# Local attention on Trainium2: the softmax matrix P transposed in one piece, with the work around it in another order

## The chip, the core and the metric

The kernel runs on one core of a Trainium2 chip. The metric is device time in microseconds (us): the median of a few executions. One further execution was profiled, and everything read from the trace comes from it.

## The reference

The input is 8 sequences of 256 tokens with 128 features. A first attention (8 heads of 16) with layer norms and a modulation comes first. Then each sequence passes six layers of local attention and a gated feed-forward block, and this is nearly all of the time:

```python
q = l2norm(q) * qs;  k = l2norm(k) * ksc          # 16 heads of 64
q = q * cos * scale + rotate_half(q) * sin * scale  # rope
k = k * cos * inv + rotate_half(k) * sin * inv
sim = einsum('bhwie,bhwje->bhwij', bq, bk2) * 8.0   # windows of 32, each sees 64 keys
attn = softmax(where(mask, -inf, sim))
x = (attn @ v) @ Wo + x
# feed-forward, 128 -> 2 x 341 -> 128
a, gate = split(layernorm(shift(x)) @ W1 + b1)
x = a * gelu(gate) @ W2 + b2 + x
```

Everything is float32 in result. The kernel gets there with matmuls in float32, and for the projections with operands split in a high and a low part (`x_hi`, `x_lo`, `wqkv_hi`, `wqkv_lo`, `w1_hi`, `w1_lo`).

## The kernel before

The six layers of eight sequences are 48 "slots" (`SLOTS`), one for each layer and sequence, numbered g. There are five programs, one for each engine: TensorE (`pe`), VectorE (`dve`), ScalarE (`act`), GpSimd (`pool`) and SyncE (`sp`, for the DMAs). Each is written out by hand, and each engine takes its instructions in this order. No scheduler moves anything; engines meet only at semaphores (`wait_ge`, `then_inc`). Waits count from `CREDIT`.

A slot has two halves, for m = 0 and m = 1, which are the two blocks of 128 tokens of the sequence. Work of several slots lies in one slot:

- attention of slot g: `scores` (TensorE), `centre` (VectorE subtracts the row maximum), `exps` (ScalarE), `turn_p` (TensorE transposes P), `copy_p` (ScalarE copies P from PSUM), `attend` (TensorE, P times V), `normalise` (VectorE), `turn_o`, `copy_o`;
- of slot g + 1 the projections `q`, `k`, `v`, their rope (`rope_products` on VectorE, `rotate` on GpSimd), the norms, and `turn_k`, `turn_q`;
- of slot g - 1 the output projection `project_out`, the `residual` and the statistics of the layer norm (`mean`, `variance`);
- of slot g - 3 (`LAG`) the feed-forward: `gates_up`, `gates`, `values_up`, `products`, `down`, `add`.

PSUM has eight banks, all in use. Banks 4 and 5 take the transposed P: in the kernel before four heads' pairs at a time (`turn_p(g, m, 0)`, then `turn_p(g, m, 1)`). The second piece goes over the first, so it waits for the copy of the first (`p_copied`). `attend` waits for the copy of the second. In the first half one half of `project_out` stands between the two pieces; in the second half `down` does.

The waits of the first half that matter here are these (lines of the kernel before):

- `k(g + 1, 0)` (L694) writes banks 6 and 7 and waits for the first of the gates, which is read from bank 7;
- `rope_products(g + 1, 0, 1)` on VectorE (L1418 and L1422) reads the projection of K and waits for `k_proj`;
- `values_up` (L857 to L864) waits for the gates and, for its last part in bank 0, for `att_done`, which the residual (L1466) gives;
- `products` (L1484) waits for the values;
- `turn_k(g, 1)` writes banks 0 and 1, so it waits for the products, and `turn_q(g, 1)` writes banks 4 and 5, so it waits for the first `normalise` (L1458), which reads `attend`'s result there:

```python
pe.wait_ge(s["f_prod"], CREDIT + 3 * (pair - LAG) + 3)     # turn_k, m = 1
pe.wait_ge(s["o_normed"], CREDIT + 2 * n - 1)              # turn_q
```

In the second half `attend(g, 1, 1)` writes banks 2 and 3 and waits for `square_of(g + 1, 1, 0)` (L1060, ScalarE), and `variance` (L833) writes bank 2 and waits for the last `normalise` of the half. At the end of a layer ScalarE also rounds the next layer's weights (`round_weights`, L990, in slots 6 and 7 of a layer; `round_up`, L995, in slot 2).

ScalarE's tables: `gates` needs the table with Gelu; the exponentials need the other. Each slot loads each once (L1157, L1159).

Of the kernel before, what the change touches and what calls it, by code (L numbers as in the profile page):

```python
# [35 lines left out]
H, D = 16, 64  # L36
INNER = H * D
W = 32
SPAN = 64
# [27 lines left out]
def build(nc, xT, w1s, w2s, w3T, woT, cT, wmod, wqkv, scales, wo, params, w1, w2, consts, out):  # L67
    with ExitStack() as ctx:
# [469 lines left out]
        def _(pe):  # L538
# [55 lines left out]
            def turn(bank, c, src):  # L594


                width = src.shape[1]
                for t in range(2):
                    r = slice(64 * t, 64 * t + 64)
                    mm = pe.transpose(ps[0:width, bank + t, 64 * c:64 * c + 64], src[r], ident[r, r],  # L600
                                      tile_position=(64 * t, 0))
                return mm
# [165 lines left out]
                                           tile_position=(D * c, W * w))  # L768
                mm.then_inc(s["scored"], 1)

            def turn_p(pair, m, g):
                n = 2 * pair + m
                if g == 0:
                    pe.wait_ge(s["centred"], CREDIT + 2 * n + 2)
                else:
                    pe.wait_ge(s["p_copied"], CREDIT + 2 * n + 1)
                pe.wait_ge(s["exped"], CREDIT + 2 * n + g + 1)
                pe.sem_inc(s["pe_waited"], 1)
                for hh in range(4):
                    mm = turn(4, hh, s_sb[:, g, 2 * hh:2 * hh + 2, :].rearrange("p c k -> p (c k)"))  # L780
                mm.then_inc(s["p_turned"], 1)

            def attend(pair, m, g, over_q=True):

                n = 2 * pair + m
                if g == 0:
                    pe.wait_ge(s["v_moved"], CREDIT + 16 * (18 * pair + 8 + 10 * m))
                    pe.wait_ge(s["p_copied"], CREDIT + 2 * n + 2)
# [14 lines left out]
                mm.then_inc(s["attended"], 1)  # L803
# [6 lines left out]
                    mm = turn(2, c, o_n[:, P * c:P * c + P])  # L810
                mm.then_inc(s["o_turned"], 1)

            def project_out(pair, half):

                if half == 0:
                    pe.wait_ge(s["o_copied"], CREDIT + 2 * pair + 2)
                    pe.wait_ge(s["w_a_loaded"], 16 * layer_of(pair) + 16)
                    pe.wait_ge(s["centred"], CREDIT + 4 * pair + 5 if not isinstance(pair, int) or pair < SLOTS - 1
                               else CREDIT + 4 * pair + 4)
                for c in range(4 * half, 4 * half + 4):  # L820
                    mm = pe.matmul(ps[:, 0, 0:N], wo_sb[:, c, :], o_t[:, c, :], start=(c == 0),  # L821
                                   stop=(c == H // 2 - 1), skip_group_check=True)
                if half:
                    mm.then_inc(s["projected"], 1)

            def mean(f, bank=1):
                pe.wait_ge(s["f_shifted"], CREDIT + 2 * f + 2)
# [58 lines left out]
            def slot(g, out=True, ff=True, ahead=True):  # L886
# [3 lines left out]
                    q(g + 1, 0)  # L890
                if ff:
                    gates_up(g - LAG)
                if out:
                    project_out(g - 1, 0)
                if ahead:
                    k(g + 1, 0, gates=ff)
                turn_p(g, 0, 0)
                if out:
                    project_out(g - 1, 1)
                turn_p(g, 0, 1)  # L900
                if ff:
                    values_up(g - LAG)
                attend(g, 0, 0)
# [9 lines left out]
                if ahead:  # L913
                    q(g + 1, 1)
                    k(g + 1, 1)
                turn_p(g, 1, 0)
                if ff:
                    down(g - LAG)
                turn_p(g, 1, 1)
                if out:  # L920
                    mean(g - 1)
                attend(g, 1, 0)
# [36 lines left out]
            project_out(SLOTS - 1, 0)  # L959
            project_out(SLOTS - 1, 1)  # L960
# [12 lines left out]
        def _(act):  # L973
# [129 lines left out]
            def copy_p(pair, m, g):  # L1103
                n = 2 * pair + m
                act.wait_ge(s["p_turned"], CREDIT + 2 * n + g + 1)
                act.wait_ge(s["attended"], CREDIT + 2 * n)
                act.activation(p_t[:, 4 * g:4 * g + 4, :].rearrange("p c (t k) -> p t c k", t=2),  # L1107
                               pair_of_banks(2)[:, :, 0:4 * SPAN].rearrange("p t (c k) -> p t c k", c=4),
                               ACT.Copy)\
                   .then_inc(s["p_copied"], 1)  # L1110

            def copy_o(pair, m):
# [40 lines left out]

            def slot(g, ff=True, norm=True, out=True, ahead=True, more=True, after=None, layer=None):

                if ff:
                    act.preload_act_table_set("gelu_and_others")  # L1157
                    gates(g - LAG)
                    act.preload_act_table_set("natural_log_exp_and_others")  # L1159
                exps(g, 0, 0)  # L1160
                if after == 7:
                    round_weights(layer, 2)
                copy_p(g, 0, 0)
                exps(g, 0, 1)
                if ahead:
                    high(g + 1, 1)
                copy_p(g, 0, 1)
                if ahead:
                    square_of(g + 1, 0, 0)
                    square_of(g + 1, 0, 1)  # L1170
# [7 lines left out]
                    inverse_norms(g + 1, 0)  # L1178

                exps(g, 1, 0)  # L1180
                if norm:
                    round_norm(g - 2)
                if after == 6:
                    round_weights(layer, 0)
                if after == 2:
                    round_up(layer)
                copy_p(g, 1, 0)
                exps(g, 1, 1)
                if more:
                    high(g + 2, 0)  # L1190
                copy_p(g, 1, 1)
                if after == 6:
                    round_weights(layer, 1)
                if ahead:
                    square_of(g + 1, 1, 0)
                if out:
# [67 lines left out]
        def _(dve):  # L1264
# [172 lines left out]
            def centre(pair, m, g):  # L1437
# [8 lines left out]
                dve.wait_ge(s["p_turned"], CREDIT + 2 * n)  # L1446
# [48 lines left out]
            def slot(g, out=True, ff=True, ahead=True):  # L1495
                centre(g, 0, 0)
                centre(g, 0, 1)
                if ahead:
                    rope_products(g + 1, 0, 0)
                    rope_products(g + 1, 0, 1)  # L1500
                if out:
                    residual(g - 1)
                if ff:
                    products(g - LAG)
                normalise(g, 0, 0)
# [139 lines left out]
```

## Time and profile before

| | |
|---|---|
| median of three executions | 1722.73 us (1717.05 to 1724.04) |
| profiled execution, its own time | 1714.45 us |
| span of the profiled execution | 1712.6 us |
| busy: TensorE, VectorE, ScalarE, GpSimd | 94%, 78%, 75%, 62% of the span |
| granted clock of TensorE, mean | 0.980 |
| chain of waits: TensorE, issue, ScalarE, VectorE | 89%, 5%, 3%, 2% of the span |
| DMA engines busy, mean | 27.3% for the main queue |

The span runs from the first to the last instruction; the execution's own time is 1.85 us more. A busy TensorE means that a matmul was running, not that it ran at its peak. The clock is a share of 2.4 GHz, and 0.5 is 1.2 GHz. The chain of waits goes back from the last instruction, at each step to what released it; when a piece of it is an engine's own instruction, the engine waited for nothing.

### The profile page before, as it was taken

The page shows a single profiled execution, that of the slowest core. Times are in us where ns is not written, and L with a number is a line of the kernel's source. Part 1 is how long each engine was busy: PE and PEld are TensorE (multiplying, and loading weights), DVE is VectorE, ACT ScalarE, POOL GpSimd, SP SyncE. Part 2 cuts the span into 40 slices and gives each one's busy share as a digit, 9 for nine tenths or more (in the row PEclk, how much of TensorE's full clock was granted, in tenths as well). Part 3 has the DMA queues.
Part 4 walks back from the last instruction along what each step waited for, and adds up shares of the span by engine and source line. Part 5 has one row for each costly group of instructions (what it writes and reads, how often), then busy time and mean ns, then how long its engine had stood idle before and what let it go on. Part 6 is the DMA issues. An engine that isn't in the chain of part 4 may idle for free.

```text
span 1712.6 us, 89331 instructions
## 1 busy us (share of the span) xinstructions
PE 1613.6 (94%) x36892; PEld 1250.3 (73%) x36892; DVE 1333.5 (78%) x1952; ACT 1282.2 (75%) x2104; POOL 1066.3 (62%) x783
## 2 busy tenths in 40 slices
PE   7896688999999999999999999999999999999996
PEld 3574567777777777777777777777777777777775
DVE  5576667787888878888888888887887888888863
ACT  4794456788787778877778777788777788787873
POOL 2202656568676768666668667678676677776641
PEclk9898899999999999999999999999999999999998
DMA  2000423222422322423322422223322222332220
GB/s 99 2 0 1 131 52 74 54 68 68 129 69 54 72 69 58 125 64 73 72 49 70 129 69 62 61 71 76 107 68 71 68 65 74 72 73 66 65 57 26
DMA packets 75728, 116.79 MB, mean 68 GB/s; under 512 B 17294, under 2 KB 27276, under 8 KB 74764
## 3 DMA queue, kind: packets, MB, share of 16 engines
q1 hardware_dynamic: 75660, 115.99, 27.3%
q8 instruction: 30, 0.49, 0.1%
q14 instruction: 38, 0.31, 0.1%
HBM read 19.04 MB, written 1.05 MB: 12 GB/s over the span
## 4 chain that ended last, share of the span: by engine, by line
PE 89%; issue 5%; ACT 3%; DVE 2%; DMA 0%; POOL 0%; ACTq 0%; DVEq 0%; SPq 0%
PE ps L600 15%; PE ps L821 10%; PE ps L714 10%; PE ps L799 9%; PE ps L764 9%; PE ps L718 8%; PE ps L717 8%; PE ps L882 4%; PE ps L757 3%; PE ps L843 2%; PE ps L845 2%; PE ps L844 2%; PE ps L833 2%; PE ps L828 2%; PE ps L589 1%
## 5 line engine op out<-in xcount | busy, mean ns | idle before, releaser
L412 POOL TENSOR_TENSOR arena<-arena,rnorm 128x1024 f32<-128x1024 f32 x192 | 361.8, 1906 | 347.6 <-ACT rnorm L1071 347.6
L403 POOL TENSOR_TENSOR arena<-arena 128x1024 f32<-128x1024 f32 x192 | 457.0, 2380 | 16.1 <-DVE arena L1422 12.4
L600 PEld LDWEIGHTS ps<-cst,arena 64*128 64x128 f32 x6656 | 243.3, 140 | 148.9 <-issue 140.1
L600 PE MATMUL ps<-cst,arena 64*128 64x64 f32 x6656 | 300.3, 230 | 25.2 <-ACT arena L1101 9.4
L1418 DVE TENSOR_TENSOR arena<-ps,rope 128x1024 f32<-128x1024 f32 x192 | 234.5, 1221 | 90.7 <-issue 79.8
L1107 ACT ACTIVATE arena<-ps 128x512 f32<-128x512 f32 x192 | 114.7, 597 | 174.3 <-PE ps L600 174.0
L1422 DVE TENSOR_TENSOR arena<-ps,rope 128x1024 f32<-128x1024 f32 x192 | 232.9, 1213 | 0.0
L718 PE MATMUL ps<-wqkv_hi,x_hi 128*128 128x512 f32 x576 | 230.0, 399 | 0.0
L717 PE MATMUL ps<-wqkv_lo,x_hi 128*128 128x512 f32 x576 | 229.4, 398 | 0.0
L1432 DVE TENSOR_REDUCE norm<-arena 128x16 f32<-128x1024 f32 x192 | 224.2, 1208 | 0.0
L714 PE MATMUL ps<-wqkv_hi,x_lo 128*128 128x512 f32 x576 | 214.8, 454 | 9.2 <-issue 7.5
L1443 DVE TENSOR_REDUCE rmax<-ps 128x8 f32<-128x512 f32 x192 | 131.7, 686 | 106.4 <-PE ps L764 105.9
L1060 ACT ACTIVATE arena<-ps 128x1024 f32<-128x1024 f32 x192 | 190.3, 1020 | 9.0 <-DVE arena L1422 9.0
L799 PE MATMUL ps<-v_sb,arena 64*32 64x66 f32 x12288 | 165.6, 227 | 26.2 <-issue 10.6
L821 PE MATMUL ps<-arena,wo_sb 128*128 128x256 f32 x768 | 186.7, 386 | 1.2 <-issue 1.2
L799 PEld LDWEIGHTS ps<-v_sb,arena 64*32 64x32 f32 x12288 | 138.1, 106 | 63.4 <-issue 52.0
L764 PE MATMUL ps<-k_t,arena 64*32 64x64 f32 x12288 | 165.7, 224 | 6.0 <-issue 6.0
L764 PEld LDWEIGHTS ps<-k_t,arena 64*32 64x32 f32 x12288 | 134.1, 105 | 29.9 <-issue 6.9
L1087 ACT ACTIVATE k_t<-ps 128x1024 f32<-128x1024 f32 x96 | 98.4, 1025 | 75.4 <-PE ps L600 73.2
L821 PEld LDWEIGHTS ps<-arena,wo_sb 128*128 128x128 f32 x768 | 139.0, 190 | 19.8 <-issue 1.3
L1447 DVE TENSOR_TENSOR arena<-ps,rmax 128x512 f32<-128x512 f32 x192 | 132.7, 691 | 15.2 <-DVE rmax L1443 0.7
L1458 DVE TENSOR_TENSOR arena<-ps,rden 128x512 f32<-128x512 f32 x192 | 132.7, 691 | 14.7
(122 smaller groups left out, 2745.4 us busy)
## 6 DMA issues: line engine op xcount, KB each, us to landing
v_sb<-v_nat SPq DMA_DIRECT2D x576, 130.0 KB, 2.4
v_sb<-v_nat SPq DMA_DIRECT2D x192, 65.0 KB, 2.0
wqkv_sb<-wqkv SPq DMA_DIRECT2D x6, 1536.0 KB, 6.4
v_sb<-v_sb SPq DMA_DIRECT2D x96, 65.0 KB, 2.0
wo_sb<-wo SPq DMA_DIRECT2D x6, 512.0 KB, 8.1
w_sb<-w SPq DMA_DIRECT2D x6, 341.0 KB, 7.8
x<-xT SPq DMA_DIRECT2D x1, 1024.0 KB, 5.0
scl<-scales SPq DMA_DIRECT2D x6, 128.0 KB, 7.6
```

What stands on the lines that cost most here:

```text
L403: pool.tensor_tensor(t_cos[:, m, j, :], t_cos[:, m, j, :], t_sin[:, j, :], ALU.add)\
L412: pool.tensor_tensor(x, x, rnorm[:, H * j:H * j + H].unsqueeze(2).to_broadcast([P, H, D]), ALU.mult).then_inc(s[done], 1)
L600: mm = pe.transpose(ps[0:width, bank + t, 64 * c:64 * c + 64], src[r], ident[r, r], tile_position=(64 * t, 0))
L714: pe.matmul(ps[:, bank + c, :], x_lo[:, m, :], wqkv_hi[:, w], start=True, stop=False)
L717: pe.matmul(ps[:, bank + c, :], x_hi[:, m, :], wqkv_lo[:, w], start=False, stop=False)
L718: mm = pe.matmul(ps[:, bank + c, :], x_hi[:, m, :], wqkv_hi[:, w], start=False, stop=True)
L764: mm = pe.matmul(ps[W * w:W * w + W, 4 * g + c, SPAN * hh:SPAN * hh + SPAN], q_t[r, 4 * g + hh, W * w:W * w + W], k_t[r, 4 * g + hh, P * m ...
L799: mm = pe.matmul(ps[W * w:W * w + W, 4 - 2 * g + c, ON * hh:ON * hh + ON], p_t[r, h, W * w:W * w + W], v_sb[r, m, w, VD * h:VD * h + ON], ...
L821: mm = pe.matmul(ps[:, 0, 0:N], wo_sb[:, c, :], o_t[:, c, :], start=(c == 0), stop=(c == H // 2 - 1), skip_group_check=True)
L1418: dve.tensor_tensor(t_cos[:, m, j, :].rearrange("p (h d) -> p h d", h=H), src.rearrange("p a (h d) -> p (a h) d", h=8), tc.unsqueeze(1).to ...
L1422: dve.tensor_tensor(t_sin[:, j, :].rearrange("p (h s d) -> p h s d", h=H, s=2), src.rearrange("p a (h s d) -> p (a h) s d", h=8, s=2)[:, : ...
L1432: dve.tensor_reduce(norm2[:, H * j:H * j + H], sq[:, j, :].rearrange("p (h d) -> p h d", h=H), AX.X, ALU.add).then_inc(s["normed"], 1)
```

## The change

P is transposed in one piece of eight pairs of heads into all of banks 4 and 5, and copied by one instruction. On TensorE this stands directly behind `gates_up`, ahead of the output projection (which is now one piece), of K and of the values; in the second half it stands ahead of `down`. On ScalarE both `exps` and the copy come first, then the gates with their two table loads, and in the second half the roundings, `high(g + 2, 0)` and `round_norm` come after the copy. On VectorE the `residual` stands ahead of the rope of K.

```diff
@@ TensorE, a slot
                 if ff:
                     gates_up(g - LAG)
+                turn_p(g, 0)
                 if out:
-                    project_out(g - 1, 0)
+                    project_out(g - 1)
                 if ahead:
                     k(g + 1, 0, gates=ff)
-                turn_p(g, 0, 0)
-                if out:
-                    project_out(g - 1, 1)
-                turn_p(g, 0, 1)
                 if ff:
                     values_up(g - LAG)
                 attend(g, 0, 0)
...
-                turn_p(g, 1, 0)
+                turn_p(g, 1)
                 if ff:
                     down(g - LAG)
-                turn_p(g, 1, 1)
                 if out:
                     mean(g - 1)
@@ TensorE, turn_p
-                if g == 0:
-                    pe.wait_ge(s["centred"], CREDIT + 2 * n + 2)
-                else:
-                    pe.wait_ge(s["p_copied"], CREDIT + 2 * n + 1)
-                pe.wait_ge(s["exped"], CREDIT + 2 * n + g + 1)
+                pe.wait_ge(s["centred"], CREDIT + 2 * n + 2)
+                pe.wait_ge(s["exped"], CREDIT + 2 * n + 2)
@@ ScalarE, a slot
+                exps(g, 0, 0)
+                exps(g, 0, 1)
+                copy_p(g, 0)
                 if ff:
                     act.preload_act_table_set("gelu_and_others")
                     gates(g - LAG)
                     act.preload_act_table_set("natural_log_exp_and_others")
-                exps(g, 0, 0)
                 if after == 7:
                     round_weights(layer, 2)
-                copy_p(g, 0, 0)
-                exps(g, 0, 1)
                 if ahead:
                     high(g + 1, 1)
-                copy_p(g, 0, 1)
...
                 exps(g, 1, 0)
+                exps(g, 1, 1)
+                copy_p(g, 1)
+                if more:
+                    high(g + 2, 0)
                 if norm:
                     round_norm(g - 2)
                 if after == 6:
                     round_weights(layer, 0)
+                    round_weights(layer, 1)
                 if after == 2:
                     round_up(layer)
-                copy_p(g, 1, 0)
-                exps(g, 1, 1)
-                if more:
-                    high(g + 2, 0)
-                copy_p(g, 1, 1)
-                if after == 6:
-                    round_weights(layer, 1)
                 if ahead:
                     square_of(g + 1, 1, 0)
@@ VectorE, a slot
                 if ahead:
                     rope_products(g + 1, 0, 0)
-                    rope_products(g + 1, 0, 1)
                 if out:
                     residual(g - 1)
+                if ahead:
+                    rope_products(g + 1, 0, 1)
                 if ff:
                     products(g - LAG)
```

On TensorE, in the first half of a slot of the main loop, this stood in a row before (L821 the output projection, L714 to L718 K, L600 the transposes of P):

```order
L821 MATMUL ps<-arena,wo_sb 128x256 x4
L696 REGISTER_ALU
L699 ISA
L714 MATMUL ps<-wqkv_hi,x_lo 128x512 x2
L717 MATMUL ps<-wqkv_lo,x_hi 128x512
L718 MATMUL ps<-wqkv_hi,x_hi 128x512
L717 MATMUL ps<-wqkv_lo,x_hi 128x512
L718 MATMUL ps<-wqkv_hi,x_hi 128x512
L774 ISA
L777 REGISTER_ALU
L600 MATMUL ps<-cst,arena 128x64 x8
L821 MATMUL ps<-arena,wo_sb 128x256 x4
```

At the same place in the changed kernel stands this (L818 is its output projection):

```order
L774 ISA
L600 MATMUL ps<-cst,arena 128x64 x16
L813 ISA
L814 ISA
L815 ISA
L818 MATMUL ps<-arena,wo_sb 128x256 x8
L696 REGISTER_ALU
L699 ISA
L714 MATMUL ps<-wqkv_hi,x_lo 128x512 x2
L717 MATMUL ps<-wqkv_lo,x_hi 128x512
L718 MATMUL ps<-wqkv_hi,x_hi 128x512
L717 MATMUL ps<-wqkv_lo,x_hi 128x512
```

The 16 transposes are in one run, and K has moved behind the whole output projection: four float32 matmuls and the transposes that stood behind it now stand ahead of it.

On VectorE, in the same half, the products of rope (L1418, L1422), the residual (L1466) and the gated products (L1484) stood so before:

```order
L1418 TENSOR_TENSOR arena<-ps,rope 128x1024
L1422 TENSOR_TENSOR arena<-ps,rope 128x1024
L1415 REGISTER_ALU
L1418 TENSOR_TENSOR arena<-ps,rope 128x1024
L1422 TENSOR_TENSOR arena<-ps,rope 128x1024
L1465 REGISTER_ALU
L1466 REGISTER_ALU x2
L1466 ISA
L1466 TENSOR_TENSOR h<-ps,h 128x256
```

In the changed kernel the lines are 13 lower:

```order
L1405 TENSOR_TENSOR arena<-ps,rope 128x1024
L1409 TENSOR_TENSOR arena<-ps,rope 128x1024
L1452 REGISTER_ALU
L1453 REGISTER_ALU x2
L1453 ISA
L1453 TENSOR_TENSOR h<-ps,h 128x256
L1402 REGISTER_ALU
L1405 TENSOR_TENSOR arena<-ps,rope 128x1024
L1409 TENSOR_TENSOR arena<-ps,rope 128x1024
```

The residual has moved from behind the second pair of rope products (K's) to ahead of it; the gated products and `normalise` follow that pair now.

## Rows read from the trace of the kernel before

**Rows 1.** Busy time in one slot: us, PE PEld DVE ACT POOL, PEclk, DMA share, GB/s.

```profile
940.36:971.05 30.69, 30.44 (x740) 24.02 (x740) 25.47 (x36) 24.05 (x39) 20.52 (x15) 1.00 0.53 149
```

**Rows 2.** The chain of waits, first half of that slot: start us, us, what.

```profile
940.36 0.24 PE ps L757 x4
...
945.17 1.73 PE ps L821 x8
...
948.30 0.39 PE ps L600 x8
948.69 1.92 PE ps L821 x8
...
951.01 0.32 PE ps L843
...
952.27 1.64 PE ps L799 x102
953.92 1.14 PE ps L600 x32
955.05 0.66 PE ps L714 x2
...
956.65 0.64 PE ps L600 x16
957.29 0.23 PE ps L757 x4
```

**Rows 3.** The chain of waits, the same slot's second half.

```profile
962.77 1.49 PE ps L882 x6
...
966.25 0.11 issue
966.36 0.85 PE ps L799 x49
...
968.35 0.66 PE ps L833 x2
...
971.05 0.23 PE ps L757 x4
```

**Rows 4.** The timeline of VectorE, first half: start us, us, instruction, idle before.

```profile
948.48 1.22 DVE L1418 TENSOR_TENSOR arena<-ps,rope 128x1024 f32<-128x1024 f32 x1 [1.80 <-issue]
...
950.93 0.42 DVE L1466 TENSOR_TENSOR h<-ps,h 128x256 f32 x1
951.96 1.26 DVE L1484 SCALAR_TENSOR_TENSOR f_a<-ps,par,f_a 128x256 f32<-128x256 f32 x3 [0.60 <-PE ps L845]
...
953.46 0.69 DVE L1458 TENSOR_TENSOR arena<-ps,rden 128x512 f32<-128x512 f32 x1
```

**Rows 5.** The timeline of VectorE, second half (first and last of 14 rows).

```profile
958.35 0.69 DVE L1443 TENSOR_REDUCE rmax<-ps 128x8 f32<-128x512 f32 x1 [0.90 <-PE ps L764]
...
967.56 0.69 DVE L1458 TENSOR_TENSOR arena<-ps,rden 128x512 f32<-128x512 f32 x1
```

**Rows 6.** The timeline of ScalarE in that slot.

```profile
942.74 1.28 ACT L1157 ACT_TABLE_LOAD   x1
944.49 0.47 ACT L1151 ACTIVATE f_a<-ps,par 85x256 f32<-85x256 f32 x1 [0.47 <-PE ps L845]
...
965.19 1.02 ACT L1060 ACTIVATE arena<-ps 128x1024 f32<-128x1024 f32 x1
```

**Rows 7.** The chain of waits, a slot that rounds weights.

```profile
902.92 1.06 ACT wqkv_hi L990
```

**Rows 8.** The timeline of TensorE, between slots 0 and 1.

```profile
215.88 1.03 PE L600 MATMUL ps<-cst,arena 64*128 64x64 f32 x27 [1.82 <-issue]
...
217.69 0.63 PE L717 MATMUL ps<-wqkv_lo,x_hi 128*128 128x512 f32 x1
```

**Rows 9.** The page's costliest groups: busy us, mean ns of one | idle before.

```profile
L717 PE MATMUL ps<-wqkv_lo,x_hi 128*128 128x512 f32 x576 | 229.4, 398 | 0.0
```

**Rows 10.** The timeline of TensorE, first slot of a loop pass.

```profile
545.67 0.46 PE L600 MATMUL ps<-cst,arena 64*128 64x64 f32 x8 [1.10 <-ACT arena L1101]
```

More of the change, by code:

```diff
@@ L769, in scores, with turn_p @@
                 mm.then_inc(s["scored"], 1)
-            def turn_p(pair, m, g):
+            def turn_p(pair, m):
                 n = 2 * pair + m
-                if g == 0:
-                    pe.wait_ge(s["centred"], CREDIT + 2 * n + 2)
-                else:
-                    pe.wait_ge(s["p_copied"], CREDIT + 2 * n + 1)
-                pe.wait_ge(s["exped"], CREDIT + 2 * n + g + 1)
+                pe.wait_ge(s["centred"], CREDIT + 2 * n + 2)
+                pe.wait_ge(s["exped"], CREDIT + 2 * n + 2)
                 pe.sem_inc(s["pe_waited"], 1)
-                for hh in range(4):
-                    mm = turn(4, hh, s_sb[:, g, 2 * hh:2 * hh + 2, :].rearrange("p c k -> p (c k)"))
+                for h in range(H // 2):
+                    mm = turn(4, h, s_sb[:, h // 4, 2 * (h % 4):2 * (h % 4) + 2, :].rearrange("p c k -> p (c k)"))
                 mm.then_inc(s["p_turned"], 1)
@@ L787, in attend @@
                     pe.wait_ge(s["v_moved"], CREDIT + 16 * (18 * pair + 8 + 10 * m))
-                    pe.wait_ge(s["p_copied"], CREDIT + 2 * n + 2)
+                    pe.wait_ge(s["p_copied"], CREDIT + n + 1)
                     pe.sem_inc(s["pe_waited"], 1)
@@ L811, in turn_o, with project_out @@
                 mm.then_inc(s["o_turned"], 1)
[L813 to L820, printed above, removed]
+            def project_out(pair):
+                pe.wait_ge(s["o_copied"], CREDIT + 2 * pair + 2)
+                pe.wait_ge(s["w_a_loaded"], 16 * layer_of(pair) + 16)
+                pe.wait_ge(s["centred"], CREDIT + 4 * pair + 5 if not isinstance(pair, int) or pair < SLOTS - 1
+                           else CREDIT + 4 * pair + 4)
+                for c in range(H // 2):
                     mm = pe.matmul(ps[:, 0, 0:N], wo_sb[:, c, :], o_t[:, c, :], start=(c == 0),
                                    stop=(c == H // 2 - 1), skip_group_check=True)
-                if half:
-                    mm.then_inc(s["projected"], 1)
+                mm.then_inc(s["projected"], 1)
             def mean(f, bank=1):
@@ L958, in _ @@
             pe.wait_ge(s["f_done"], CREDIT + SLOTS - LAG)
-            project_out(SLOTS - 1, 0)
-            project_out(SLOTS - 1, 1)
+            project_out(SLOTS - 1)
             down(SLOTS - 3, 7)
@@ L1101, in exps, with copy_p @@
                 act.activation(v, v, ACT.Exp).then_inc(s["exped"], 1)
-            def copy_p(pair, m, g):
+            def copy_p(pair, m):
                 n = 2 * pair + m
-                act.wait_ge(s["p_turned"], CREDIT + 2 * n + g + 1)
+                act.wait_ge(s["p_turned"], CREDIT + n + 1)
                 act.wait_ge(s["attended"], CREDIT + 2 * n)
-                act.activation(p_t[:, 4 * g:4 * g + 4, :].rearrange("p c (t k) -> p t c k", t=2),
-                               pair_of_banks(2)[:, :, 0:4 * SPAN].rearrange("p t (c k) -> p t c k", c=4),
-                               ACT.Copy)\
+                act.activation(p_t.rearrange("p c (t k) -> p t c k", t=2),
+                               pair_of_banks(2).rearrange("p t (c k) -> p t c k", c=8), ACT.Copy)\
                    .then_inc(s["p_copied"], 1)
@@ L1445, in centre @@
                 dve.wait_ge(s["maxed"], CREDIT + 2 * n + g + 1)
-                dve.wait_ge(s["p_turned"], CREDIT + 2 * n)
+                dve.wait_ge(s["p_turned"], CREDIT + n)
                 dve.tensor_tensor(s_sb[:, g, :, :].rearrange("p (h a) k -> p a h k", a=2), src,
```

## The prediction

> **What bounds the kernel now.** I read the granted clock and the busy time of one slot first, then the chain of waits through it, then the timelines of VectorE and ScalarE beside it. In the steady part TensorE is busy for 30.44 of a slot's 30.69 us at full clock [rows 1]. The chain of waits goes from scores to scores (940.36 to 971.05) nearly always through TensorE's own instructions; the first half takes 957.29 - 940.36 = 16.93 us, the second 13.76 [rows 2, 3]. So TensorE is the bound, with little waiting in it. What the chain doesn't say is how near the others are, and this change moves what the others wait for. That is what has to be worked out: where TensorE gets shorter, and which engine is then late.
>
> **What TensorE saves.** P is turned in two pieces, each between two full-array jobs. A run of 8 transposes takes 0.39 us, of 16 0.64 (turn_o), of 32 1.14 [rows 2]: 0.14 us to enter and 0.031 for each. The float32 passes behind transposes take 1.92 us for 8 (half an output projection) and 1.49 for 6 (down) [rows 2, 3], thus 0.215 a pass and 0.20 to enter; the same 8 passes behind another full matmul take 1.73. The values' first matmul takes 0.32 behind transposes, where I take 0.12 behind a full one. Joining the pieces removes one entry of each kind in each half: 0.14 + 0.20 = 0.34, say 0.35 us. If that were all, the first half would be 16.58 us.
> The Trainium skill (TensorE: Matmul & The Clock Gate, "Step-by-step: what each phase is for") says that weight loads are pulled ahead of running matmuls unless their row groups conflict. By that alone the joints could be free and the saving zero; the 1.92 against 1.73 us [rows 2] says that they are not, and the row decides.
>
> **The first half: who is late.** Count from the end of gates_up (945.17). On TensorE, in the new order: 16 transposes 0.64, the whole output projection 1.92 + 8 x 0.215 = 3.64, K 948.30 - (945.17 + 1.73) = 1.40: K is ready at +5.68, where it was ready at +3.13. Behind it: values 1.26 - 0.20 = 1.06, attend 1.65, and turn_k would begin at +8.39 and turn_q, 16 transposes later (0.64), at +9.03.
> VectorE can only begin K's rope products when K is there. It began 0.18 us after K's end (948.48 against 948.30); the pair takes 2.45 us to the next instruction (950.93); the three gated products begin at 951.96 and last 1.26; the first normalise behind them is over at 953.46 + 0.69 = 954.15, that is 2.19 us after the products' start [rows 4]. Before, the residual and the wait for the values lay between; there the gated products ended at 953.22 and TensorE came to turn_k only at 953.92: 0.7 us of slack. Now nothing lies between, but all of it begins 2.55 us later. With 0.10 us for the signal ([rows 3]: 0.11 of "issue" before attend's second piece):
> - products ready for turn_k at 5.68 + 0.18 + 2.45 + 1.26 + 0.10 = +9.67, against +8.39 that TensorE would need: it waits 1.28 us;
> - normalise ready for turn_q at 5.68 + 0.18 + 2.45 + 2.19 + 0.10 = +10.60, against +9.03: 1.57 us late in all (0.3 of it after turn_k).
> From there 0.50 (the second 16 of 32 transposes), v 956.65 - 955.05 = 1.60 and turn_o 0.64 lead to the scores at +13.34. They were at 957.29 - 945.17 = +12.12. So the first half gets 1.22 us longer: 0.35 saved, 1.57 lost.
> The residual ahead of the rope costs nothing: the projection ends at +4.28, the residual takes 0.42 [rows 4], and it lies in VectorE's wait for K. The delay of K is the price, not the residual.
> P's own chain is short enough. Centre begins 1.06 us behind the start of the scores (958.35 against 957.29) [rows 2, 5] and takes four instructions of 0.69; the last exponential is half as wide as the 1.02 us of the square [rows 6], so some 0.6. That is 4.5 us, and gates_up ends at 945.17 - 940.36 = 4.81, because ScalarE no longer loads a table ahead of it. I put the wait at 0; with signals it could be up to 0.2, and it would count in full.
>
> **The second half.** The same joint saves 0.35 us of TensorE. But VectorE works there from 958.35 to 967.56 + 0.69 = 968.25 with no idle note on the 13 rows after the first [rows 5], and variance, which waits for its last instruction, begins at 968.35 [rows 3]. VectorE's work is tied to the scores and is not made shorter. So at most 0.05 us is gained, whatever TensorE saves; the bounds are 0 and 0.35. I take 0.05, the row's.
>
> **What is special.** Five slots round two pieces of weights. A 1024-wide rounding takes 1.06 us [rows 7]. Before, one was hidden in ScalarE's wait for P and one was on the path; now both stand ahead of the square that attend's second piece waits for: I count 0.8 us for each slot, 4 us (0 to 5). The six slots that round W1 get 0.3 each, 2 us (0 to 4). Slots 1 and 2, which have no feed-forward, also have K behind the projection: 1 us each. The last slot has no K and loses two waits for P: -3 (0 to -4). DMAs: none is added, and v's moves are tied to copy_v, which keeps its distance to the scores.
>
> **Sum.** 44 slots (3 to 46) x (1.22 - 0.05) = 51.5; with 4 + 2 + 2 - 3 = 5 it is 56.5 us. From the profiled execution's 1714.45 us this gives 1771. The median of the runs shown is 8 us above that execution; I go half of the way and say 1776 us, 3% slower. (What a measurement can tell from no change is about 0.5%, 8 us.)
>
> **The rivals.**
> 1. *TensorE's saving counts and VectorE does not hold it.* That is what the chain of waits by itself suggests, since it is nearly all TensorE. Then 45 slots x 0.70 = 31 us go: 1684 to 1692 us. Against it: rope products can't read K before K is there, and the 2.45 + 2.19 us behind it are measured. It would need VectorE to get there 1.6 us earlier. 8%.
> 2. *Saving and wait cancel.* For a change within 8 us a slot may gain or lose 0.18 us, so the wait would have to be 0.2 to 0.6 us, and not 1.57: 1715 to 1730 us. Even with turn_k's wait alone and the whole second joint saved it is 1.28 - 0.70 = 0.58 a slot, 26 us, 1740; that is the low end of my forecast, not this rival. 5%.
> 3. *The clock falls too.* TensorE gets pauses of 1.3 and 0.3 us in each slot. After a pause of 1.82 us the matmuls of the projection take 0.63 us, where they take 0.40 in the mean [rows 8, 9]: this is the lower level, 1.2 GHz. After one of 1.10 us the transposes run at the full one [rows 10]: 0.46 us for 8. The new pauses lie between. A fall costs about 1.7 us (0.2 us on each of eight or nine such matmuls; that so many are hit is an estimate, from the stretch between those two slots). One slot in three: 15 x 1.7 = 25 us, 1800; each slot: 75 us, 1850. 13%. The Trainium skill (TensorE: Matmul & The Clock Gate, "HAM oscillation — how this bites in real kernels") describes this: a loop with a wait in each pass may begin every pass at the lower clock. [...]
> 4. *The gates get late.* They stand behind the copy of P and a table load now, and K waits for the first. P turned at +0.64, copied in 1.02 [rows 6], table 1.28, first gate 0.47: +3.5 with the signals, while K can begin at +4.28. There is 0.8 us of slack. If it were used up, K would come later, and each 0.1 us of it costs 4 us. 4%, about 1790.
>
> **Chances and range.** My forecast 70% (1750 to 1800), rivals 1 to 4: 8, 5, 13 and 4%. Faster by over 0.5%: 8%; within 0.5%: 5%; slower: 87%. The range from 1742 takes in rival 2's 26 us and no special slots at the low end, and up to 1806 a fall of the clock in a slot of three; beyond it lie rival 1 and the worse part of 3, about 2 in 10.
>
> **What would show it.** In the profile after: the first half 18.1 to 18.2 us between the scores, the second 13.7; transposes of P in runs of 16 with 0.64 us; K's rope products starting 0.2 us after K, and the gated products directly behind them; VectorE as releaser ahead of turn_k and turn_q with about 1.3 and 0.3 us; in the chain VectorE's share far above its 2%; ScalarE's gates over before K begins. The granted clock stays at 1.00 in the steady part; lower values there would speak for rival 3. The prediction is wrong if TensorE does not wait ahead of turn_k, or if the first half is under 17 us.

## The result and the profile after

The changed kernel takes 1768.7 us (1764.8 to 1775.1, four runs), the kernel before 1719.9 us on the same chip: a ratio of 1.030, with a 95% interval of 1.027 to 1.033. It is 3% slower, and the forecast was 1776 (1742 to 1806). The profiled execution took 1767.6 us, its span is 1765.8, and the mean granted clock 0.978.

Slot times below are differences between starts of the first scores of each half, on TensorE's timeline. They repeat within 0.03 us in the plain slots:

| us | before | after | after - before |
|---|---|---|---|
| first half, plain slot | 16.93 | 18.11 | +1.18 |
| second half, plain slot | 13.76 | 13.67 | -0.09 |
| second half, slots 14, 22, 30, 38 (two roundings) | 14.82 | 16.8 | +2.0 |
| second half, slots 10, 18, 26, 34, 42 (W1) | 13.76 | 14.15 | +0.4 |
| first half, slots 11, 19, 27, 35 (first of a loop pass) | 18.4 to 18.6 | 19.6 to 19.8 | +1.2 |
| slots 0 to 3 together | | | -7.5 |

The 53.2 us by which the span grew are 43 slots (4 to 46) by 1.09 = 46.9, 8.8 more in the five slots that round two pieces of weights, 2.4 in those that round W1 and 0.5 in the others; slots 0 to 3 give 7.5 back, the start costs 2.5 and the end gives 0.4. The fifth of the slots with two roundings is slot 6: it went from 14.82 to 15.36 us only (see experiment 6).

Busy times of one plain slot of the kernel after (slot 24), in the columns of [rows 1]:

```profile
962.93:994.71 31.78, 30.09 (x743) 24.35 (x739) 25.31 (x36) 24.28 (x37) 20.51 (x15) 1.00 0.51 144
```

TensorE's busy time fell from 30.44 to 30.09 us while the slot grew to 31.78: its work got shorter, and it now waits 1.69 us. The chain through the first half of that slot says where, to be read against [rows 2]:

```profile
967.78 0.64 PE ps L600 x16
968.42 3.65 PE ps L818 x16
972.07 0.47 PE ps L714 x2
...
973.24 0.24 PE ps L718
...
975.92 1.26 DVE f_a L1471 x3
977.19 0.25 issue
977.44 0.71 PE ps L600 x16
978.16 0.71 PE ps L600 x16
978.87 0.66 PE ps L714 x2
...
980.46 0.64 PE ps L600 x16
981.10 0.23 PE ps L757 x2
```

P is turned in 0.64 us, the projection takes 3.65, K begins at 972.07. Then the chain leaves TensorE: it goes through VectorE's rope products (many small pieces and "issue", left out here) to the three gated products (975.92) and back to TensorE's transposes of K at 977.44 and of Q at 978.16, each 16 of them in 0.71, where 32 took 1.14 in one go before. VectorE's timeline of the slot, to be read against [rows 4, 5]:

```profile
972.39 0.42 DVE L1453 TENSOR_TENSOR h<-ps,h 128x256 f32 x1 [3.09 <-PE ps L818]
973.65 1.22 DVE L1405 TENSOR_TENSOR arena<-ps,rope 128x1024 f32<-128x1024 f32 x1 [0.84 <-PE ps L718]
974.79 1.22 DVE L1409 TENSOR_TENSOR arena<-ps,rope 128x1024 f32<-128x1024 f32 x1
975.92 1.25 DVE L1471 SCALAR_TENSOR_TENSOR f_a<-ps,par,f_a 128x256 f32<-128x256 f32 x3
977.10 0.19 DVE L1442 RECIPROCAL rden<-ps 128x8 f32<-128x8 f32 x1
977.32 0.69 DVE L1445 TENSOR_TENSOR arena<-ps,rden 128x512 f32<-128x512 f32 x1
...
982.16 0.69 DVE L1430 TENSOR_REDUCE rmax<-ps 128x8 f32<-128x512 f32 x1 [0.84 <-PE ps L764]
...
990.21 0.20 DVE L1442 RECIPROCAL rden<-ps 128x8 f32<-128x8 f32 x1
990.45 0.69 DVE L1445 TENSOR_TENSOR arena<-ps,rden 128x512 f32<-128x512 f32 x1
...
991.29 0.69 DVE L1445 TENSOR_TENSOR arena<-ps,rden 128x512 f32<-128x512 f32 x1
```

VectorE is idle for 3.09 us ahead of the residual and 0.84 ahead of K's rope. From there on it has no gap up to the second half's row maximum at 982.16, which waits 0.84 us for the scores, and none behind that to the end of the half. Before, it waited 0.60 us for the values ahead of the same products. The waits of TensorE (engine, line, releaser, us in total, times, longest):

```profile
PE ps L600 <- DVE f_a L1471: 51.1, 44, 1.3
PE ps L797 <- ACT arena L1051: 30.7, 46, 2.3
```

The first is the new wait: 1.24 to 1.27 us in the plain slots, 1.16 in the mean, since it is only 0.5 in the five slots that round a third piece of weights. Before, the largest wait of TensorE in that list was 10.6 us in all. The second was not foreseen: attend's second piece waits for a square of ScalarE in each second half, 0.37 us in the plain slots, 1.03 where W1 is rounded and 2.26 where two pieces are. The 0.37 cost nothing: in experiment 6 the square comes earlier, this wait is gone, and the half takes the same 13.67 us. In the page's chain TensorE's share fell from 89 to 71%:

```profile
PE 71%; issue 9%; DVE 8%; ACT 7%; POOL 2%; DVEq 1%; ACTq 1%; DMA 0%; SPq 0%; POOLq 0%
```

ScalarE in the first half, against [rows 6]:

```profile
968.54 1.02 ACT L1098 ACTIVATE arena<-ps 128x1024 f32<-128x1024 f32 x1 [0.98 <-PE ps L600]
969.58 1.28 ACT L1150 ACT_TABLE_LOAD   x1
970.87 1.20 ACT L1141 ACTIVATE f_a<-ps,par 85x256 f32<-85x256 f32 x3
```

The gates end at 972.07, when K begins; K waits for the first of the three only.

### The profile page after: what moved, and what is told of

Read it like the earlier page. It is cut to its first block, busy times and chain, and to the rows that moved or that the text cites. A ratio compares the mean times of both kernels' runs of the same rounds, so it can differ in the third digit from the quotient of the medians.

```text
span 1765.8 us, 88923 instructions
## 1 busy us (share of the span) xinstructions
PE 1599.6 (91%) x36892; PEld 1267.7 (72%) x36892; DVE 1326.8 (75%) x1952; ACT 1291.2 (73%) x2008; POOL 1065.7 (60%) x783
## 3 DMA queue, kind: packets, MB, share of 16 engines
HBM read 19.04 MB, written 1.05 MB: 11 GB/s over the span
## 4 chain that ended last, share of the span: by engine, by line
PE 71%; issue 9%; DVE 8%; ACT 7%; POOL 2%; DVEq 1%; ACTq 1%; DMA 0%; SPq 0%; POOLq 0%
PE ps L600 14%; PE ps L818 10%; PE ps L714 9%; PE ps L764 8%; PE ps L718 7%; PE ps L717 7%; DVE f_a L1471 3%; PE ps L797 3%; DVE arena L1409 2%; PE ps L757 2%; ACT arena L1051 2%; PE ps L829 2%; PE ps L589 2%; ACT f_hi L1132 1%; PE ps L839 1%
## 5 line engine op out<-in xcount | busy, mean ns | idle before, releaser
L600 PEld LDWEIGHTS ps<-cst,arena 64*128 64x128 f32 x6656 | 246.8, 141 | 164.8 <-issue 149.6
L600 PE MATMUL ps<-cst,arena 64*128 64x64 f32 x6656 | 294.4, 231 | 75.6 <-DVE f_a L1471 51.1
L1051 ACT ACTIVATE arena<-ps 128x1024 f32<-128x1024 f32 x192 | 195.3, 1017 | 58.6 <-DVE arena L1409 56.9
L718 PE MATMUL ps<-wqkv_hi,x_hi 128*128 128x512 f32 x576 | 228.8, 397 | 0.0
L714 PE MATMUL ps<-wqkv_hi,x_lo 128*128 128x512 f32 x576 | 215.1, 455 | 7.8 <-issue 7.2
L1092 ACT ACTIVATE arena<-arena 128x512 f32<-128x512 f32 x192 | 121.1, 633 | 96.8 <-DVE arena L1434 81.9
L818 PE MATMUL ps<-arena,wo_sb 128*128 128x256 f32 x768 | 180.3, 388 | 1.2 <-issue 1.2
L1098 ACT ACTIVATE arena<-ps 128x1024 f32<-128x1024 f32 x96 | 98.4, 1025 | 107.0 <-PE ps L600 107.0
L818 PEld LDWEIGHTS ps<-arena,wo_sb 128*128 128x128 f32 x768 | 143.2, 191 | 22.3 <-issue 1.3
```

Of the source, the lines that this page charges most:

```text
L714: pe.matmul(ps[:, bank + c, :], x_lo[:, m, :], wqkv_hi[:, w], start=True, stop=False)
L718: mm = pe.matmul(ps[:, bank + c, :], x_hi[:, m, :], wqkv_hi[:, w], start=False, stop=True)
L1051: act.activation(sq[:, j, :], pair_of_banks((1, 3)[j]).rearrange("p a b -> p (a b)"), ACT.Square).then_inc(s["squared"], 1)
```

## The experiments

Each edit is shown against the kernel named with it, and against the kernel after where none is named. The kernel before took 1717.3 us beside experiments 1 to 4, 1714.2 beside 5 to 8 and 1715.7 beside 9 to 11.

**1. K ahead again, the joint of the first half alone.** The output projection is in two halves, and P is turned in one piece between them; the second half is that of the kernel before.

```diff
                 if out:
-                    project_out(g - 1)
+                    project_out(g - 1, 0)
                 if ahead:
                     k(g + 1, 0, gates=ff)
+                turn_p_all(g, 0)
+                if out:
+                    project_out(g - 1, 1)
```

> The kernel before, with P in one piece in the first half alone and K where it was: output projection's first half, K, 16 transposes of P, second half of the projection, values. Both exponentials stand ahead of the gates, the copy of P behind them; the second half of the slot and VectorE's order are as before. Theory (K's delay is the whole loss, the joint a real saving): K is ready at +3.1 us after gates_up as before, the gated products are over before TensorE reaches turn_k, and the first half gets shorter by the joint: 16.93 - 0.35 = 16.58 us, second half 13.76; 44 slots x 0.35 = 15 us less, about 0.99 of before. Rival (the single piece itself, or the exponentials ahead of the gates, costs): the first half stays over 16.9 us or nears 18.1.

Measured: 1731.2 us, ratio 1.010 (1.007 to 1.013). The plain first half took 17.06 us, the second 13.76. So 1.05 of the 1.18 us came back. This kernel differs from the kernel after in the place of the residual and in ScalarE's order too, so by itself it does not single out K's place; experiments 3 and 4 and the chain do. The joint brought nothing here, against the 0.35 us of the theory. The projection ended later than before, the residual began at 607.29, and the values' last part waited for it (TensorE went on at 607.77):

```profile
607.29 0.43 DVE L1481 TENSOR_TENSOR h<-ps,h 128x256 f32 x1 [0.35 <-PE ps L830]
```

It also has one thing that neither theory holds: the first slot of each loop pass took 22.3 to 22.5 us, where ScalarE stood still for 4.76 us with nothing to wait for in the records:

```profile
536.56 1.15 ACT L1109 ACTIVATE arena<-arena 128x512 f32<-128x512 f32 x2 [4.76 <-issue]
```

The same slots took 18.5 us before; four of them are 15 us, as much as this kernel's whole distance to the kernel before.

**2. The joint of the second half alone.** The first half is that of the kernel before, the second that of the kernel after.

```diff
-                turn_p(g, 1, 0)
+                turn_p_all(g, 1)
                 if ff:
                     down(g - LAG)
-                turn_p(g, 1, 1)
```

> The kernel before with only the second half of the slot changed as in the changed kernel (P in one piece ahead of down, exponentials and copy first, roundings and high behind them). Theory: first half 16.93 us as before; second half 13.67 as in the changed kernel, bound by VectorE's unbroken work and not by TensorE (which alone would give 13.41); in the four slots that round weights after the first layer, ScalarE's two roundings hold attend's second piece and the second half is 16.8 us instead of 14.8. Sum about -3.5 us for the plain slots, +10 for the rounding ones, some +3 for W1's: 5 to 10 us above before. Rival (the first half's delay also shapes the second half): 13.7 and 16.8 would not appear here.

Measured: 1734.2 us in one execution, 17 above before where 5 to 10 were expected; plain slots 16.92 and 13.75. The slots with two roundings took 15.4 to 17.0 us in the second half, as expected in the main. The joint gives the plain second half nothing, not even the 0.09 us of the kernel after that the theory had forecast. What gives those is on VectorE. With P in two pieces in either half, the count of its copies is two for each half, and the program holds a register instruction between the first reciprocal and the multiplication behind it:

```text
194 L1455 RECIPROCAL rden<-ps 128x8 [waits attended]
195 L1457 REGISTER_ALU [waits recip]
196 L1458 TENSOR_TENSOR arena<-ps,rden 128x2x4x64 [waits o_turned]
```

It is gone in the kernel after. These are the two rows of the kernel before, to be read against 990.21 and 990.45 above:

```profile
966.40 0.20 DVE L1455 RECIPROCAL rden<-ps 128x8 f32<-128x8 f32 x1
966.72 0.69 DVE L1458 TENSOR_TENSOR arena<-ps,rden 128x512 f32<-128x512 f32 x1
```

From the reciprocal's start to the multiplication's it took 0.32 us before, 0.32 to 0.33 in this experiment, and 0.24 after. VectorE has no slack in the second half, so this one instruction is the whole gain. The first slots of the loop's passes took 20.8 to 23.6 us here, nearly as in experiment 1. That is 14 us more than before, which the theory did not have.

**3. K's rope made shorter, in the kernel after.** Half of the heads of K's sine product are left out in the first half of a slot.

```diff
+                hs = H // 2 if (m == 0 and j == 1) else H
```

> The changed kernel, with VectorE's sine product of K's rope in the first half computed for 8 of 16 heads only (the other heads keep stale values). The instruction gets about 0.57 us shorter. Theory (the path is K, rope products, gated products, normalise, turn_q): the whole first half gets shorter by the same 0.57 us: 18.11 to 17.55; 44 to 46 slots, about -26 us. Rival (ScalarE's late gates and squares, or TensorE itself, hold the half): under 0.1 us a slot.

Measured: 1739.8 us in one execution; plain first half 17.57 (0.54 less), second 13.67. The instruction went from 1.22 to 0.68 us on VectorE, and the slot gets all of the 0.54. This is the most direct proof that K's rope sets the first half after.

**4. The same edit in the kernel before.**

> The same cut in the kernel before: K's sine product of the first half for 8 of 16 heads. Theory: VectorE has 0.7 us of slack there ahead of turn_k, so nothing changes: 16.93 us and the time of before within 0.2%. Rival (VectorE bounds the kernel before too): up to 0.5 us a slot, 25 us.

Measured: 1713.2 us in one execution; plain slots 16.91 and 13.77. The same instruction was covered there. Between the two kernels it went from worth nothing to worth 1:1.

**5. K early, P in one piece behind the projection, the roundings apart.** Here the parts are put where experiments 1 to 4 say that they have room. The gates are ahead of the exponentials and the residual is behind K's rope again, as before; the diff shows only a part of the edit.

```diff
+                if out:
+                    project_out(g - 1, 0)
                 if ahead:
                     k(g + 1, 0, gates=ff)
+                if out:
+                    project_out(g - 1, 1)
+                turn_p(g, 0)
...
                 exps(g, 1, 0)
+                if norm:
+                    round_norm(g - 2)
                 exps(g, 1, 1)
+                if after == 6:
+                    round_weights(layer, 0)
                 copy_p(g, 1)
```

> The kernel after, with three things put otherwise: in the first half the output projection is issued in two halves with K between them, as before, and P is turned in one piece behind the second half; the gates stand ahead of the exponentials; the residual follows K's rope products; in the second half P stays in one piece, and the roundings of weights and of the norm are spread between the exponentials and behind the square instead of standing together. Theory (K's place set the loss, and the joint of P by itself is worth 0.35 us of TensorE): the plain first half 16.58 us against 16.93 before and 18.11 after, the second 13.67, also in the slots with roundings; that is 0.44 us a slot under before, about 20 us in 44 slots and 6 from the rounding slots: 1690 us (1685 to 1700) if ScalarE's stall in the first slot of a loop pass stays at its 2.5 us, up to 1712 if it is 5 us as in the first experiment. Rival (the joint brings no time on the chip, VectorE follows whatever TensorE does): first half 16.9, 1712 to 1725 us.

Measured: 1689.4 us (1688.5 to 1695.3), ratio 0.986 (0.982 to 0.990). It beats both kernels. Plain slots took 16.72 and 13.66 us, and the slots with two roundings 13.65; the slots behind them took 13.9. Of the joint's gain 0.21 us arrived and not 0.35. The chain of waits shows both numbers:

```profile
961.02 0.47 PE ps L714 x2
...
962.42 1.73 PE ps L819 x8
964.14 0.64 PE ps L600 x16
964.78 0.32 PE ps L841
...
966.04 0.84 PE ps L797 x49
966.88 0.11 issue
966.99 0.85 PE ps L797 x49
967.85 1.14 PE ps L600 x32
968.99 0.66 PE ps L714 x2
...
970.57 0.64 PE ps L600 x16
971.21 0.23 PE ps L757 x4
```

From K's end to the values it is 964.78 - 962.42 = 2.36 us, where [rows 2] have 951.01 - 948.30 = 2.71: the 0.35 of the prediction. Of it 0.11 is lost in the "issue" at 966.88, ahead of attend's second piece.

**6. The kernel after, with the roundings apart.** The second half of ScalarE is put as in experiment 5, nothing else.

> The kernel after, in which only the roundings on ScalarE in the second half are spread (round_norm between the exponentials, one of the weights' pieces ahead of the copy of P and one behind the square). Theory (ScalarE is late for the square in the rounding slots, and the long pause of TensorE there is what brings its clock down): the second half of slots 14, 22, 30 and 38 falls from 16.8 us to 13.7 to 14.5, of slots 10, 18, 26 and 34 from 14.15 to 13.7, no stretch of the steady part under a granted clock of 1.00 but for the loop's wraps; together 10 to 16 us, 1753 to 1758. Rival (the second half there is held by VectorE or a DMA of the weights): no change, 1768.

Measured: 1748.1 us in one execution. The second half took 13.67 us in every slot from 4 on, and the granted clock is 1.00 throughout the slots that round: the roundings cost nothing when they stand in ScalarE's waits. By slots the kernel after loses (16.8 - 13.67) x 4 + 1.7 (slot 6) + 0.48 x 5 = 16.6 us to them; the whole differs by 20, of which some 3 lie ahead of slot 4 and behind slot 46. In the kernel after, slot 22 looks like this on TensorE:

```profile
921.96 0.86 PE L797 MATMUL ps<-v_sb,arena 64*32 64x66 f32 x64
925.08 1.05 PE L797 MATMUL ps<-v_sb,arena 64*32 64x66 f32 x64 [2.26 <-ACT arena L1051]
926.06 1.97 PE L600 MATMUL ps<-cst,arena 64*128 64x64 f32 x32
```

and in a stretch of it (the columns of [rows 1]):

```profile
925.08:929.10 4.02, 4.02 (x99) 3.55 (x100) 2.89 (x4) 2.10 (x3) 4.02 (x3) 0.58 0.14 33
```

ScalarE rounds for 1.99 us ahead of the square, TensorE pauses for 2.26, and the granted clock is 0.58 in the mean of the stretch behind it, most of which is at the lower level of 1.2 GHz: 32 transposes take 1.97 us and not 1.14 to 1.21. Slot 6 parts the two costs. It has the same pause of 2.26 us, its clock stayed at 1.00, and it took 15.36 us: so of the 3.1 us the pause is 1.7 and the fall of the clock 1.4.

**7. The kernel after, with the residual late.** It stands behind K's rope products again.

```diff
                     rope_products(g + 1, 0, 0)
+                    rope_products(g + 1, 0, 1)
                 if out:
                     residual(g - 1)
-                if ahead:
-                    rope_products(g + 1, 0, 1)
```

> The kernel after, with the residual back behind K's rope products on VectorE. Theory: with K behind the whole projection the residual must lie in VectorE's wait for K; put back, the values' third part waits for it, and attend and all behind it come 0.5 to 1.1 us later in each first half: 18.6 to 19.2, 1790 to 1815 us. The second half stays at 13.67. Rival (the residual's place makes no difference, since its 0.44 us fit anywhere): 18.11, 1768 us.

Measured: 1853.4 us in one execution, far past the range. In slots 5, 17, 21, 34 and 39 the first half took 19.0 us, as expected; in the others 20.0 to 20.4 (21.5 to 21.9 in the first of a loop pass). The values' last part waits for the residual, as theory had it:

```profile
880.32 0.38 PE L839 MATMUL ps<-f_hi,w_lo 128*128 128x256 f32 x1 [2.22 <-DVE h L1453]
...
880.87 1.93 PE L797 MATMUL ps<-v_sb,arena 64*32 64x66 f32 x128
882.73 1.97 PE L600 MATMUL ps<-cst,arena 64*128 64x64 f32 x32
```

What theory lacked is the clock. These are TensorE's busy time and granted clock behind the pause in slot 20, and at the same place of slot 21:

```profile
882.00:884.60 2.60, 2.60 (x91) 0.52 0.00 0
914.00:916.69 2.69, 2.26 (x133) 1.00 0.00 0
916.69:917.83 1.14, 1.14 (x34) 1.00 0.00 0
```

In slot 20 the granted clock was 0.52 in the mean of that stretch (nearly all of it at the lower level), and the 32 transposes took 1.97 us; in slot 21, after an equal wait, it stayed at 1.00, and they took 1.14. That is the 1.0 to 1.4 us between 19.0 and the rest. So this part of the change was needed: given K behind the whole projection, the residual ahead of the rope saves some 85 us (one execution against the kernel after's median), about half of it by the wait and half by the clock.

**8. The kernel after, its code moved.** 16 activations of one element stand ahead of ScalarE's main loop.

```diff
+            for i in range(16):
+                act.activation(norml[0:1, i:i + 1], par[0:1, L_BG:L_BG + 1], ACT.Copy)
```

> The kernel after, with 16 activations of one element each (a copy into a buffer that is written anew) ahead of ScalarE's main loop: under 3 us of work outside the loop, and nothing changed within it. Theory A (ScalarE's stall at the wrap of the outer loop depends on where the loop's instructions lie in memory): the wrap slots' first half changes from its 19.7 us by 1 us or more. Theory B (it depends on what stands in the loop, or on the transfers under way at that time): 19.6 to 19.8 as before the shift, and the whole 1768 to 1772 us.

Measured: 1771.1 us in one execution; wrap slots 19.6 to 19.7. ScalarE's stall there was 2.56 to 2.68 us, against 2.58 to 2.81 after and 2.42 to 2.61 before. Moving the code by 16 instructions doesn't change it, so this move gives no support to theory A.

The traces say more of this stall. The queue that the profile calls "instruction" has a packet of 8 KB in every one of them: in all 13 profiles, four wraps in each, it starts 0.74 to 0.79 us into the stall (once 1.07), and ScalarE goes on 1.2 to 1.5 us after the last such packet is over. In the 44 stalls of 2.4 to 2.8 us there is one packet, in the 8 of experiments 1 and 2 there are two. So the stall is most likely a wait for instructions to be loaded, and a long one two loads in a row; that the packets are ScalarE's own is argued from their times, the trace does not name their engine.

**9. Experiment 5, with one square ahead of the copy of P.**

```diff
                 if after == 7:
                     round_weights(layer, 2)
+                elif ahead:
+                    square_of(g + 1, 0, 0)
                 copy_p(g, 0)
```

> The kernel of the fifth experiment, in which ScalarE squares the next query ahead of the copy of P in the first half (save in the one slot of eight that rounds weights there), in the 1.74 us in which it waits for P. Theory (of the 0.33 us that the joint takes from TensorE in the first half, 0.11 are lost where attend's second piece waits for ScalarE, whose copy of P now begins 0.5 us later than the second half-copy did): plain first half 16.60 instead of 16.72, second unchanged at 13.66; about 4.5 us in 38 slots, 1685 us (1681 to 1688). Rival (VectorE's products are next, 0.1 us behind): 16.68 to 16.72, no change.

Measured: the plain first half took 16.62 us, and the small "issue" ahead of attend's second piece is gone (one run of matmuls, before two with a gap):

```profile
940.38 1.69 PE ps L797 x98
942.08 1.14 PE ps L600 x32
```

The theory of the loss holds. The whole doesn't show it: 1689.8 us, ratio 0.986 (0.983 to 0.988), no different from experiment 5, where 0.1 us in 38 slots would be 4. In the profiled executions slots 0 to 3 took 136.3 us here and 130.2 there. Those slots differ from kernel to kernel, and why was not looked into.

**10. Experiment 5, with the rope of the second half shorter.** Half of the heads of K's sine product are left out in the second half.

> The kernel of the fifth experiment, leaving out half of the heads of K's sine product in the second half only (their values then stay those of earlier; about 0.57 us less of VectorE a slot). Theory (VectorE, at work without a gap from the scores to the second normalise, holds the second half): it falls from 13.66 us to 13.25 to 13.45, then held by TensorE, and the whole by 10 to 18 us to 1672 to 1680. Rival (ScalarE's square or TensorE itself holds it): 13.66, 1689.

Measured: 1666.2 us in one execution, below the forecast; the second half went from 13.66 to 13.18 us, with the first at 16.7. VectorE was the bound of the second half, and the others could do it in 0.48 us less.

**11. Experiment 5, with the roundings together.**

> The kernel of the fifth experiment, with the roundings of the second half put together again, as in the kernel after. Theory: plain slots stay at 16.72 and 13.66; the second half of slots 14, 22, 30 and 38 goes to 16.5 to 17, of slots 10, 18, 26 and 34 to 14.15, together 14 to 17 us: 1704 to 1707. Also whether the first slot of a loop pass keeps 18.4 us: in the first two experiments, where these roundings stood together too, it was 22 to 23. If that place makes ScalarE's stall 5 us instead of 2.6, another 15 to 20 us come on top, 1722.

Measured: 1708.5 us in one execution; slots 14 and 10 had 16.83 and 14.18 us in the second half, slots 6 and 22 15.38, without a fall of the clock. The wrap slots stayed at 18.1 to 18.2. So the roundings' place is worth 15 us here in slots 4 to 46; of the 21 us by which the span is longer than in experiment 5, 5.6 lie in slots 0 to 3 (135.8 us against 130.2) and are not explained. It isn't what made ScalarE stall for 5 us in experiments 1 and 2.

## Why the prediction was right

- *TensorE saves 0.35 us a half.* Right as TensorE's work: its busy time in a slot fell by 0.35 (the two halves would give 0.70, but the 32 transposes of K and Q take 1.42 us where they took 1.14, which leaves 0.42), and experiment 5 shows 0.35 in the chain.
- *K is ready at +5.68, turn_k begins at +9.67, the scores at +13.34.* Counted from gates_up's end (967.78) they came at 973.48, 977.44 and 981.10: +5.70, +9.66 and +13.32. TensorE's wait was 1.27 us in most plain slots, 1.28 forecast. Turn_q began at +10.38, not +10.60, and then took 0.71 us and not 0.50, so that it was over at +11.09, 11.10 forecast. The path is right; that it agrees to 0.01 us is luck. The pair of rope products took 2.27 us to the next instruction (973.65 to 975.92) and not 2.45, which was measured up to the residual, and the signal to turn_k 0.25 and not 0.10. The pause of 0.3 us ahead of turn_q did not show as a wait of its own.
- *The first half gets 1.22 longer.* It got 1.18. Experiments 3 and 4 show the cause: 0.54 us less of K's rope is 0.54 us less of the slot here and nothing in the kernel before. With K early, in experiment 1, 1.05 of it is gone.
- *The second half gains at most 0.05.* It gained 0.09, and VectorE is the bound (experiment 10, in the kernel of experiment 5). The step's reason for the 0.05 was wrong: no joint was in it (experiment 2), but one register instruction on VectorE.
- *The residual costs nothing.* Right, and more: it was needed (experiment 7).
- *The roundings cost 4 us.* This term was mis-sized, at less than half: 8.8 beyond the plain slots' change, and 16.6 against what is possible (experiment 6). Of it 4 x 1.4 = 5.6 us are the fall of the clock in four of the five slots, which had not been counted. W1's 2 came to 2.4.
- *Slots 1 and 2 cost 2, the last slot gives 3.* They came to +1.1 and to less than 1. These terms were small, and slots 0 and 3 moved more, by -8.6 us, which no step foresaw. The 51.5 us of the plain slots came to 46.9 in 43 of them, so a part of the total's nearness is luck: less here and in slots 0 and 3, more in the roundings and ahead of slot 0.
- *Rival 3, the clock.* It fell nowhere in the plain slots, with pauses of 1.27 us, and did so in four of the five slots with 2.26. The Trainium skill (TensorE: Matmul & The Clock Gate, "HAM oscillation — how this bites in real kernels") has a loop whose every pass begins slow, and the wait in each pass of that loop is about 3 to 5 us. It does not say that a pause of 1.3 us costs anything, and here none did. Experiment 7, with a pause of 2.22 us in each slot, came near to that picture: all but 5 of the 43 slots from 4 to 46 paid.
- *Rival 4, the gates.* K began with no wait noted, while the third gate was just ending; it needs only the first.

The sum itself, 1771 us, was nearer than the 1776 given: the median of the changed kernel lay 1 us above its profiled execution, not the 5 that were added.

## What to carry to other kernels

Joining two short pieces of work on the busiest engine saves their entries only. What stands between them moves too, and here that was K, which the second engine of the slot was waiting for. So before moving an instruction on the bound engine, count from it the whole chain on the other engine, up to the place where the first engine waits again; the order that wins keeps the early product early and puts the joined piece where only slack is (experiment 5).

Small extra work on an engine with slack is free only inside its waits. Put together in one place, 2 us of roundings made a pause that in four slots of five brought the clock down, and then cost 3.1 us and not 1.7.

## What the runs showed of the hardware

- Pauses of TensorE of 1.24 to 1.27 us in each slot left the granted clock at 1.00, and in slots 4 to 46 of all 13 profiles no pause of 0.6 to 1.6 us that stood alone was followed by the lower level. Behind pauses of 2.2 to 2.3 us it came in most cases and not in all: 4 of 5 in the kernel after and in experiment 2, 2 of 5 in experiment 3, 3 of 5 in experiment 11, 5 of 5 in experiment 8, 43 of 48 in experiment 7. Behind those of 2.5 to 2.9 us in experiment 2 it came twice in four. Behind the four of 3.6 to 3.9 us in experiment 1 it came each time. Each fall behind a pause of 2.2 to 2.3 us cost 1.0 to 1.4 us. Why equal pauses differ stays open.
- One register instruction between a reciprocal and the multiplication that needs it costs 0.08 to 0.09 us on VectorE.
- ScalarE stands still at the wrap of the long loop, without a releaser in the records: 2.4 to 2.8 us in 11 of the 13 kernels, with one 8 KB packet of the instruction queue in the stall, and 4.7 to 5.2 in experiments 1 and 2, with two. It was not the place of the roundings (experiment 11), nor did moving the code by 16 instructions change it (experiment 8). What decides between one packet and two stays open; experiments 1 and 2 share P's two-piece code beside the one-piece code, which no other kernel here has, and this was not tried by itself.
